# Part 0 of a four-stage transformer kernel takes in one more batch of the first attention, on one core of a Trainium2 chip

## What is computed

```
x = norm(x + attention0(x))      # 16 heads of 64, softmax over 256 keys, output projection
x = norm(x + ffn0(x))            # routing: 8 clusters of 8 tiles, argmax by gates, spline, table rows
x = norm(x + attention1(x))      # a linear attention and a windowed one (16 heads of 8), a gate between
x = norm(x + ffn1(x))            # attention in 128-token halves (16 heads of 64, causal), then 8 experts of 128 x 512
```

## Time and profile before

| | us |
|---|---|
| median of 3 runs (lowest, highest) | 2451.48 (2449.78, 2452.81) |
| the profiled execution, its own time | 2448.45 |
| its span, first to last instruction | 2446.7 |
| part 0 | 0 to 214.8 |
| part 1 | 214.8 to 507.8 |
| each of parts 2 to 7 | about 293 |
| part 8 | 2266 to 2446.7 |

### The profile page before, as it was taken

One profiled execution on the slowest core, in us unless ns is written; L12 is line 12 of the kernel. 1 busy time (PEld: TensorE's weight loads), 2 busy tenths in 40 slices (PEclk: granted clock), 3 DMA queues, 4 the chain that ended last, 5 costly groups with the idle time before them and its releaser, 6 DMA issues.

```text
span 2446.7 us, 43966 instructions
## 1 busy us (share of the span) xinstructions
PE 2219.9 (91%) x16096; PEld 1544.8 (63%) x16096; DVE 1570.6 (64%) x4247; ACT 1366.2 (56%) x3798; POOL 848.0 (35%) x1010
## 2 busy tenths in 40 slices
PE   7758998999989999999999999899998989999797
PEld 5545656756668566675666765676666756667465
DVE  4566676576656766667665767657676676666742
ACT  4436573755647655476555756465563764546442
POOL 2313461045510544106431256113561054510630
PEclk9878999999999999999999999999999999998899
DMA  4000000000010000110001000000001000010001
GB/s 145 27 1 1 1 10 27 18 31 1 10 35 10 31 10 1 44 31 2 10 1 44 32 1 10 18 27 31 1 10 33 13 31 1 1 35 10 31 1 48
DMA packets 24561, 50.43 MB, mean 21 GB/s; under 512 B 3285, under 2 KB 3869, under 8 KB 23965
## 3 DMA queue, kind: packets, MB, share of 16 engines
q1 hardware_dynamic: 24348, 47.62, 6.0%
HBM read 45.52 MB, written 2.10 MB: 19 GB/s over the span
## 4 chain that ended last, share of the span: by engine, by line
PE 71%; DVE 14%; POOL 6%; issue 5%; ACT 4%; DVEq 0%; ACTq 0%; POOLq 0%
PE ps L1439 9%; PE ps L1460 9%; PE ps L865 5%; PE ps L638 5%; PE ps L833 4%; PE ps L1396 4%; PE ps L655 4%; PE ps L1379 3%; PE ps L1472 3%; PE ps L593 3%; PE ps L1336 3%; PE ps L1347 3%; PE ps L747 3%; PE ps L764 2%; PE ps L800 2%
## 5 line engine op out<-in xcount | busy, mean ns | idle before, releaser
L1005 POOL TENSOR_TENSOR rstd<-ve,half_neg 128x4 f32<-128x4 f32 (+1 forms) x56 | 66.9, 1194 | 1016.1 <-DVE ve L986 1016.1
L1460 PEld LDWEIGHTS ps<-wbuf,QK 128*128 128x128 f32 x2048 | 265.4, 191 | 108.9 <-issue 101.6
L1259 POOL TENSOR_TENSOR E<-E,ri 128x512 f32<-128x512 f32 x240 | 248.3, 1041 | 192.8 <-DVE ri L1058 192.7
L1563 ACT ACTIVATE QK<-ps,cols 128x512 f32<-128x512 f32 x256 | 172.9, 686 | 219.0 <-PE ps L1439 218.6
L888 ACT ACTIVATE E<-ps,nm 128x256 f32<-128x256 f32 x480 | 224.7, 481 | 107.7 <-DVE nm L1051 106.8
L1439 PE MATMUL ps<-h2T,wbuf 128*128 128x512 f32 x512 | 277.9, 632 | 0.2
L1460 PE MATMUL ps<-wbuf,QK 128*128 128x128 f32 x2048 | 269.0, 275 | 0.2
L1689 POOL TENSOR_TENSOR work<-work,ri 128x128 f32<-128x128 f32 x480 | 231.4, 508 | 103.5 <-DVE ri L1612 103.3
L1682 POOL TENSOR_TENSOR rn<-ss,half_neg 128x8 f32<-128x8 f32 x120 | 195.7, 1638 | 168.7 <-DVE ss L1588 167.8
L1523 ACT ACTIVATE work<-ps,nm 128x128 f32<-128x128 f32 x480 | 198.9, 427 | 73.8 <-DVE nm L1603 72.6
L1051 DVE TENSOR_REDUCE nm<-ps 128x2 f32<-128x512 f32 x256 | 168.8, 684 | 65.2 <-PE ps L638 64.1
(11 more groups left out here) (279 smaller groups left out, 4537.3 us busy)
## 6 DMA issues: line engine op xcount, KB each, us to landing
wbuf<-in_w SPq DMA_DIRECT2D x128, 256.0 KB, 3.2
xT<-in_xT SPq DMA_DIRECT2D x8, 256.0 KB, 2.7
xr<-in_xr SPq DMA_DIRECT2D x8, 256.0 KB, 3.0
bias_t<-in_bias_t SPq DMA_DIRECT2D x1, 2048.0 KB
out_y<-xn SPq DMA_DIRECT2D x8, 256.0 KB, 2.1
wqkv<-in_wqkv SPq DMA_DIRECT2D x1, 1536.0 KB
wo<-in_wo SPq DMA_DIRECT2D x2, 512.0 KB, 8.8
rows<-in_rows SPq DMA_DIRECT2D x1, 531.0 KB, 7.1
```

The lines of the kernel that those rows point to most:

```text
L1259: nc.gpsimd.tensor_tensor(L.E[:, g % 4, :, :], L.E[:, g % 4, :, :], L.ri[:, g, :].unsqueeze(2).broadcast_to((P, NT, S)), ALU.mult)\
L1460: last = nc.tensor.matmul(bank2[2 + x % 2][:, t * P:(t + 1) * P], hid[:, x % 2, c, t * P:(t + 1) * P], w2[:, x % WB, c, :], start=(c == 0) ...
```

## The change

Part 0 takes in one more batch. After batch 1 of pair 0, the second lane also runs the whole first attention (projection, 16 heads, output projection) of **batch 0 of pair 1**. Its output is copied from PSUM to `acc`, which the experts do not use in part 0. `ahead_pe` of part 0 now projects batch 1 of pair 1, not batch 0. Part 1 adds `acc` to its input at its start, and its first lane then has heads of one batch only, batch 1, whose projection is there already. All else of part 1 stays: routing chain, window stage, and the whole second half.

Part 1 has a kind and tables of its own (`second_part`). All other tables (`first`, `both`, and `last`, which was `second`) are written anew as well. In the heads of ffn1 the masks and the scores of a round are now two steps for the tables instead of one. SP issues the load of the next pair's input after six expert loads of a part instead of three (in part 1, after seven).

The core of the diff:

```
-KINDS = ["first", "both", "both", "second"]
+KINDS = ["first", "second_part", "both", "both", "last"]
...
                     if u == 0 and n:
-                        pe.wait_ge(s["y1_ready"], upto("y1_ready", n))
+                        pe.wait_ge(s["y1_ready"], upto("y1_ready", n if L.tag == "1" else NP))
+                        if L.tag == "2":
+                            pe.wait_ge(s["x_next"], upto("x_next", 32))
                     first_proj(pe, L.bank[u % 3], b, u).then_inc(sem_of(L, "proj"), 1)
...
+        def early_pe(pe):
+            yield from first_heads_pe(pe, first_b, 1, 0, 0)
+            yield from first_heads_pe(pe, first_b, 0, 1, 1)
...
             if both:
-                yield from first_heads_pe(pe, first_a, 0, 0, None)
-                yield from first_heads_pe(pe, first_a, 1, 1, 0)
+                if p == 1:
+                    yield from first_heads_pe(pe, first_a, 1, 0, None)
+                else:
+                    yield from first_heads_pe(pe, first_a, 0, 0, None)
+                    yield from first_heads_pe(pe, first_a, 1, 1, 0)
...
             dve.wait_ge(sem_of(L, "wo_done"), upto("wo_done" + L.tag, n + 1))
+            if L.tag == "2" and n:
+                nc.vector.tensor_copy(acc[:, 0:NT, :], tri(L.bank[0][:, 0:S], 2)).then_inc(s["early_ready"], 1)
+                return
...
+                if p == 1:
+                    yield
+                    dve.wait_ge(s["xb_ready"], upto("xb_ready", 1))
+                    nc.vector.tensor_tensor(y1[:, 0:NT, :], acc[:, 0:NT, :], xb[:, 0:NT, :], ALU.add)\
+                        .then_inc(s["y1_ready"], 1)
+                    yield from first_heads_dve(dve, first_a, 1, 0, None)
...
-                        pe.wait_ge(s["y1_ready"], upto("y1_ready", NP))
+                        pe.wait_ge(s["early_ready"], upto("early_ready", 1))
                 if u >= 3:
                     pe.wait_ge(s["pre_copied"], upto("pre_copied", u - 2))
-                first_proj(pe, bank2[u % 3], 0, u).then_inc(s["pre_proj"], 1)
+                first_proj(pe, bank2[u % 3], 0 if p else 1, u).then_inc(s["pre_proj"], 1)
```

More of the change, by code:

```diff
@@ L69 @@
[L69 to L74 removed]
+        "0001100101110011000111010101010100111111011011101101100010",
@@ L87 @@
     ("both", "sync"):
-        "1110111111",
-    ("second", "vector"):
-        "000000000000001000111111101001110110110101110011111011110111111110000111111000001110000001000101"
-        "111000010111100001011101000101111000100111100001011100100011111000100111100000111000110010000000"
+        "1111110111",
+    ("last", "vector"):
+        "000000000000010000111111101001111100110111101001111011111111011110011000111100001110000000001101"
+        "111010000111100010011110000011101110000111010000111110000001111100010111100000111000110010000000"
@@ L101 @@
+    ("last", "scalar"):
+        "000000000010111110011000111001111111111111000000001111000011110000111100001111000011110000111100"
+        "001111000011111000001110000000000000000000000000000000000000",
+    ("last", "gpsimd"):
+        "000011101101110011010100110010110001101010110100000",
 }
-KINDS = ["first", "both", "both", "second"]
+KINDS = ["first", "second_part", "both", "both", "last"]
 def merged(order, *programs):
@@ L427, in whole_net @@
         COUNT.update(dict.fromkeys("""
+            exp2
+        """.split(), (64, 64, 64, 64, 32)))
+        COUNT.update(dict.fromkeys("""
             dve1
-        """.split(), (61, 61, 61, 0)))
+        """.split(), (61, 61, 61, 61, 0)))
         COUNT.update(dict.fromkeys("""
-            exp1 exp2
-        """.split(), (32, 64, 64, 32)))
+            exp1
+        """.split(), (32, 32, 64, 64, 32)))
+        COUNT.update(dict.fromkeys("""
+            ri2 norm2 w_trn2
+        """.split(), (32, 32, 32, 32, 16)))
@@ L898, in first_heads_act, with early_act, first_act @@
                             .then_inc(sem_of(L, "et_act"), 1)
-        def first_act(act, both):
-            if both:
-                yield from first_heads_act(act, first_a, 0, 0, None)
-                yield from first_heads_act(act, first_a, 1, 1, 0)
+        def early_act(act):
+            yield from first_heads_act(act, first_b, 1, 0, 0)
+            yield from first_heads_act(act, first_b, 0, 1, 1)
+        def first_act(act, p):
+            both = p > 0
+            if both:
+                if p == 1:
+                    yield from first_heads_act(act, first_a, 1, 0, None)
+                else:
+                    yield from first_heads_act(act, first_a, 0, 0, None)
+                    yield from first_heads_act(act, first_a, 1, 1, 0)
             else:
@@ L1261, in first_heads_pool, with early_pool, first_pool @@
                     .then_inc(sem_of(L, "norm"), 1)
-        def first_pool(pool, both):
+        def early_pool(pool):
+            yield from first_heads_pool(pool, first_b, 1, 0)
+            yield from first_heads_pool(pool, first_b, 0, 1)
+        def first_pool(pool, p):
+            both = p > 0
             yield
@@ L1269, in first_pool @@
             if both:
-                yield from first_heads_pool(pool, first_a, 0, 0)
-                yield from first_heads_pool(pool, first_a, 1, 1)
+                if p == 1:
+                    yield from first_heads_pool(pool, first_a, 1, 0)
+                else:
+                    yield from first_heads_pool(pool, first_a, 0, 0)
+                    yield from first_heads_pool(pool, first_a, 1, 1)
             else:
```

205 lines of the change are left out of this document (121 added, 84 removed).

## The result

The changed kernel has a median of 2428.79 us (2427.33 to 2430.0, four runs) against 2450.63 for the kernel before. The ratio is 0.991 with a 95% interval of 0.9893 to 0.9927.

The account below looks back on a forecast made before the run. PE was taken as the main bound (71% of the chain that ended last), with DVE carrying part 0's routing chain. 24 - 17.2 + 0 = +6.8 us, on 2448.45 plus 3.03, gave 2458 us, range 2437 to 2475.

Parts of the forecast that it names:

- Parts 2 to 8: Later parts, where only the tables differ: no change, with 0.6 us a part to either side.
- own sign of being wrong: Among the signs that the forecast is wrong: a later part moves by over 1 us.
- The rival on the tables: New tables matter in parts 2 to 8, 1 us each, 7 us in all: 2451 or 2465; no chance given.
- Part 0: +24: Part 0 with the added batch gets 24 us longer, with ends of about +12 and +38.
- (a): Part 0's routing chain: the added batch's DVE instructions between chain instructions delay it, +14.5 us, from 9 to 18.
- (d): Part 0's routing chain: thirteen POOL normalizes of 1.04 us hold up DVE, +3 us; 13.5 if all block fully.
- rival of full blocking: Two-input DVE instructions wait out each POOL normalize: 13.5 us instead of 3, time 2469; chance 0.15.
- (c): Part 0's window stage: 9.8 us of added PE work lengthens it by +7 us, from 4 to 10.
- (e): Part 0's PE clock: a busier PE may be granted more clock, -2 us, with ends 0 and -10.
- (b): Start of part 0's chain: six projection matmuls on PE ahead of its first transposes, +1.5 us, from 0 to 4.
- Part 1: -17.2: Part 1 without the moved batch: heads 18.5 us shorter, 1.3 added by a DVE wait; ends -33 and -7.
- one rival: Whole kernel: gain and loss cancel to within 0.2% (4.9 us), 2447 to 2456 us; chance 0.20.

Follow-up runs that it names:

- tables_only: The kernel before, without the batch's move, with the new tables in parts 1 to 8; 2420.23 us, ratio 0.9878 to the kernel before.
- the thinned kernels: The changed kernel with POOL's normalizes, or DVE's maxima and copies, of part 0's added batch cut to few columns; 2419.07 and 2419.13 us.
- keep_warm_after: The changed kernel with two matmuls whose results nobody reads added to each of parts 1 to 7; 2416.6 us, ratio 0.9857 to the kernel before.
- part1_thin: The changed kernel with part 1's first-lane scores and weights times values on 64 of 256 columns; 2430.23 us, ratio 0.9900 to the kernel before.
- keep_warm_part1: keep_warm_after with five more matmuls without a reader in part 1, where PE waits in the second lane's first batch; 2413.31 us.
- move_only: The changed kernel with the tables of before in parts 2 to 8; 2451.69 us, ratio 0.9999 to the kernel before.

## Why the prediction was wrong

**Parts 2 to 8: 0 with 0.6 us a part.** This is the step that failed. "Only the tables differ ... The work is the same and both stages of a part are PE's, so 0" took a PE that is busy 149.99 of 157.50 us as one that no order can help. In parts 2 to 7 the new tables gave 24.3 us, 12.3 of idle time and 12.0 of clock. `tables_only` gave 30 us without the move, and one digit of PE's table 16.5 of the 25.0 us that they gave in parts 2 to 7. The prediction's own sign of being wrong, a later part that moves by over 1 us, came out in all of parts 2 to 7 (2.0 to 5.9 us). The rival on the tables had the place right and the price wrong: 1 us a part instead of 4, and it was set beside the cases without a chance of its own. The list of PE at a part's start stood in the order and was not read; only the three places of the move were.

**Part 0: +24.** The sign and the place were right. It was 17.3 us: 0.9 before the chain, 14.0 in it (60.30 to 74.25) and 2.5 behind it (60.4 to 62.88).
- (a) DVE in the chain, +14.5. Thinning 20 of the 30 instructions should have given the chain back 9.6 us and gave 5.6. So an instruction cost the chain some 0.6 of its length. That the rest was covered where the chain waited for something else fits this, but was not shown instruction by instruction.
- (d) POOL against DVE, +3 with an end at 13.5. It was 5.0 in the chain. The 3.9 us behind it are no part of this, since an unthinned part 0 had them too. The estimate was too small, and the rival of full blocking had the mechanism right for an instruction and too many of them. Together (a) and (d) are 10.6 of the chain's 14.0 us if they add up; the other 3.4 were not taken apart.
- (c) and (e), the window stage at +7 and the clock at -2. In the chain the clock rose from 0.63 to 0.91, which shortened it little, as the 75.7 us at 0.80 show. Behind it the clock rose from 0.87 to 0.92. The rest of part 0 took on 5.7 us of PE busy time (53.50 to 59.17) for 2.5 us of length. At full clock, in the thinned kernels and in `keep_warm_after`, it took 59 us, which is less than before the change. So +7 was too much because the added work was laid, in full, on a stage that had been running at 0.87 and could get faster; that -2 for the clock was too small a price for it is the likely reason, and no run holds the clock fixed to show it.
- (b) was not measured apart.

**Part 1: -17.2.** It was -11.9. The second lane's scores show the rounds:

```profile
L1462 PE MATMUL ps<-QK x64: 272/376/631, 264.2 to 298.5; 64*128 64x128 f32 x32, 64*128 64x256 f32 x32
```

```profile
L1462 PE MATMUL ps<-QK x64: 272/374/378, 336.8 to 371.6; 64*128 64x128 f32 x32, 64*128 64x256 f32 x32
```

By the arithmetic of the earlier trace rows a round takes (298.5 - 264.2 - 0.8)/7 = 4.8 us and (371.6 - 336.8 - 0.8)/7 = 4.9, against 4.7 and 5.4 before. The claim that the moved work does not come off in full was right: from scores to the end it is 47.4 and 49.2 us (45 and 46 forecast), the rest is 50.7 (48 forecast), in sum 147.3 instead of 139. The gap before the experts, where +1.3 was forecast, came out 1.6 shorter. What the sum left out is the clock. It stood at 0.99 in the heads before, and at 0.90 and 0.87 in the first two of these four stretches. PE's waits alone don't tell where it falls: in the third PE is idle for 5.0 of 28 us at a clock of 1.00.

```profile
238.70:264.00 25.30, 19.60 (x66) 9.04 (x66) 16.87 (x33) 9.17 (x18) 13.03 (x8) 0.90 0.00 1
264.00:309.00 45.00, 39.06 (x275) 24.68 (x274) 23.52 (x67) 24.83 (x103) 23.41 (x40) 0.87 0.00 1
309.00:337.00 28.00, 23.01 (x112) 12.89 (x112) 20.45 (x41) 11.63 (x28) 14.98 (x10) 1.00 0.00 1
337.00:385.00 48.00, 42.72 (x345) 28.64 (x346) 27.12 (x81) 25.85 (x99) 22.34 (x39) 1.00 0.01 1
```

PE's busy time of part 1 fell by 26.0 us (273.0 to 247.0), where 38.8 of work left. In `part1_thin`, 12.4 us less work saved nothing by the medians, and the profiled execution took 6.7 us more in part 1, at a lower clock. `keep_warm_part1` gave back 2.4 us. How the remaining 3 us divide between waits for exps and clock stays open.

**The move as a whole.** Forecast at +6.8, measured +5.4 in the profiles, 0 to 2 us by `move_only`, and 8 by `tables_only` against the changed kernel. Gain and loss nearly cancel, as one rival said. The experts' stage did not change, as forecast.

**The sum.** The 29.5 us between 2458.3 and 2428.8 are 24.3 from parts 2 to 7 less 0.4 from part 8, 1.4 from the move, and 4.2 from the term that took the median 3.03 us above the profiled execution: in the changed kernel it lies 1.2 below.

## What to carry to other kernels

When a change rewrites an order table, compare the whole list of the bounding engine, beginning with every place where it waits: an instruction that is ready and stands behind one that is not can cost a wait and, on TensorE, the clock after it, which here was the larger share. Price work on TensorE at the clock of its own stage, and ask of any work taken away whether the idle time it leaves lowers that clock. Before a difference of 1% in one stage is explained, look at a stage whose program is the same in several profiles: part 0 alone differed by 3 us. Small VectorE instructions that read SBUF beside GpSimd's passes over SBUF can cost the pass's remaining time and not their own, as two of them did here; those that read PSUM kept their time.

## What was not expected of the hardware

- TensorE's clock fell to the lower of its two levels after waits of 1.80 and 0.87 us, and the dip outlasted the waits: 0.53 over the 3.5 us behind a part's start. With one wait shortened by 1.1 us it was gone. Identical parts with identical lists took 287.5 or 291.3 us for this reason alone.
- Two matmuls a part without a reader, 1.1 and 0.6 us long, made the whole 12 to 14 us faster. Two variants with more of them gave 3 us and nothing.
- In the profiled execution of a kernel with 12.4 us less matmul work in part 1, a stretch of that part ran at a clock of 0.77 instead of 0.87, and the part took 6.7 us more. By the medians the work taken out was worth nothing.
- A VectorE step on 32 elements took 0.93 us instead of 0.18 beside a GpSimd multiply of 1.04 us.
